# A state-space block with an expert layer: the scan in sub-chunks of 64 tokens, and where B is turned

## What is computed

```python
x = silu(_causal_conv(input_tensor @ Wx.T, conv_w, conv_b))
b = (x @ Wb.T).reshape(bsz, seq, HEADS, STATE)
c = (x @ Wc.T).reshape(bsz, seq, HEADS, STATE)
dt = softplus(x @ Wdt.T + b_dt)
def step(state, inp):
    x_t, b_t, c_t, dt_t = inp
    decay = exp(dt_t * a)[..., None, None]
    state = decay * state + (dt_t[..., None] * b_t)[..., None] * x_t[:, :, None, :]
    return (state, einsum('bhn,bhnp->bhp', c_t, state))
```

## Time and profile before

| | before |
|---|---|
| median of 3 runs | 1219.45 us |
| lowest, highest | 1218.78, 1220.4 us |
| span of the profiled execution | 1219.8 us |
| granted TensorE clock, mean | 1.000 |
| TensorE busy | 1203.0 us, 99% |
| VectorE busy | 951.8 us, 78% |
| GpSimd busy | 791.4 us, 65% |
| ScalarE busy | 714.7 us, 59% |

### The profile page before, as it was taken

The page is one execution under the profiler, slowest core; times in us unless marked ns, Lnnn a source line. Parts: engine busy times, 40 slices in busy tenths (PEclk is TensorE's granted clock), DMA queues, the critical chain, the costliest instruction groups (busy, mean ns, idle before and its releaser), DMA issues.

```text
span 1219.8 us, 30709 instructions
## 1 busy us (share of the span) xinstructions
PE 1203.0 (99%) x11883; PEld 993.8 (81%) x11883; DVE 951.8 (78%) x2027; ACT 714.7 (59%) x1465; POOL 791.4 (65%) x788
## 2 busy tenths in 40 slices
PE   8999999999999999999999999999999999999998
...
GB/s 300 252 343 341 289 242 140 114 136 120 134 140 117 136 126 122 141 129 119 134 135 122 136 124 169 175 156 92 111 91 92 98 87 127 261 324 321 332 332 167
DMA packets 112351, 214.28 MB, mean 176 GB/s; under 512 B 20432, under 2 KB 78544, under 8 KB 107600
## 3 DMA queue, kind: packets, MB, share of 16 engines
...
...
## 4 chain that ended last, share of the span: by engine, by line
PE 86%; DVE 5%; DMA 3%; SPq 2%; ACT 2%; issue 1%; POOL 1%; ACTq 0%; DVEq 0%; POOLq 0%
PE ps L1439 27%; PE ps L1801 10%; PE ps L2311 8%; PE ps L2290 7%; PE ps L2075 6%; PE ps L1520 4%; PE ps L1487 3%; PE ps L2077 3%; PE ps L1546 3%; PE ps L1509 3%; PE ps L1531 2%; PE ps L1560 2%; PE ps L690 1%; PE ps L743 1%; DMA parts_dram<-xn_lo 1%
## 5 line engine op out<-in xcount | busy, mean ns | idle before, releaser
L1395 ACT ACTIVATE decay<-tap,ncum 128x128 f32<-128x128 f32 x344 | 105.7, 392 | 141.4 <-POOL tap L1289 141.4
L1985 POOL DMA_INDIRECT ffn_dram<-ob,idx x64 | 108.4, 1694 | 85.8 <-DVE ob L1904 74.6
L1296 POOL TENSOR_TENSOR x_lo<-x,x_hi 128x512 fp32r<-128x512 f32 x56 | 77.3, 1380 | 104.3 <-ACT x_hi L1368 104.3
L1174 DVE TENSOR_TENSOR x_dt<-ps,dt 128x512 f32<-128x512 f32 x64 | 44.3, 691 | 120.3 <-PE ps L1546 120.3
L2075 PE MATMUL ps<-dn,mid_hi 128*128 128x512 f32 x288 | 104.9, 399 | 0.5 <-DVE moments L1875 0.5
L2033 ACT ACTIVATE mid<-ps,b_up 128x512 f32<-128x512 f32 x96 | 65.9, 690 | 67.2 <-PE ps L1801 56.3
L1439 PE MATMUL ps<-x_hi,w_hi_b 128*128 128x512 f32 x240 | 99.4, 414 | 0.0
L1439 PE MATMUL ps<-x_hi,w_hi_c 128*128 128x512 f32 x240 | 99.3, 414 | 0.0
L2166 POOL TENSOR_SCALAR yc<-yc,gn_scale,gn_shift 128x512 f32<-128x512 f32 x56 | 76.5, 1378 | 33.0 <-DMA yc<-y_dram 32.9
L1439 PE MATMUL ps<-x_lo,w_hi_b 128*128 128x512 f32 x240 | 94.4, 393 | 0.0
L1439 PE MATMUL ps<-x_lo,w_hi_c 128*128 128x512 f32 x240 | 94.2, 393 | 0.0
...
...
## 6 DMA issues: line engine op xcount, KB each, us to landing
...
```

The costliest lines, as they stand in the source:

```text
L1296: nc.gpsimd.tensor_tensor(low, raw, high, ALU.subtract).then_inc(x_lo_ready, 1)
L1395: n = nc.scalar.activation(decay[g % 2][:, h, :], cum_row[g % NR][:, row, :], ACT.Exp, bias=t.ncum[:, g, h:h + 1])
L1985: pool.indirect_dma_start(out=t.ffn_dram, out_offset=bass.IndirectOffsetOnAxis(ap=t.idx[:, e, h * HC + c:h * HC + c + 1], axis=0), in_=ob[ ...
```

## The change

The scan now works in sub-chunks of 64 tokens, two a chunk. Only the two diagonal quarters of a head's 128x128 matrix are left in `scores` and `own_parts`: 16 products of 64 columns each. What the lower quarter carried goes through the state, which steps twice a chunk: `state_mid` after the first half, the other state tile after the second. So `state_parts` runs twice with 64 columns (8 products each), and `update` makes 16 products of 64 rows, one set for each half, into the free half of the scores' banks. On VectorE `mix` becomes one instruction of 512 elements; the four folding instructions become `shrink` (a state tile times decays, both in SBUF) and an addition, once for each half; the two additions into `yb` become one of 512 elements and two of 128.

Order: x of the next chunk is turned at the head of a chunk, B of the next chunk behind the C projection, and `update` of the next chunk follows its scores. On VectorE `weigh_b` is now the last thing in a chunk. `x_dt` has two buffers. The exchange of halves goes away everywhere (`turned_pair` and its uses), as do the split copies in the front; `update` no longer waits for the bit search or the experts' banks. The front gains four products that sum the decays of each half, and cumulates over 64 tokens. `load_cum` issues four DMAs of 128 KB for one of 512 KB, and two more stores fill `cum_half_dram`. The causal mask takes two GpSimd instructions for three, `exp_rows` one ScalarE instruction for two. The first sub-chunk of a sequence needs no state; every other one has state parts, and `update` and the turn of B now also run for the last chunk of a sequence.

```diff
@@ phase_front, TensorE
-            pe.matmul(ps_t[1][:, 0:NT * H], t.ones, flat, start=True, stop=True).then_inc(ten, 1)
+            pe.matmul(ps_t[1][:, 0:NT * H], t.later, flat, start=True, stop=True).then_inc(ten, 1)
+            for j in range(2):
+                for a in range(2):
+                    mm = pe.matmul(ps_dt[a * s.HD:(a + 1) * s.HD, j * NT * MT:(j + 1) * NT * MT],
+                                   t.headavg[:, j * s.HD:(j + 1) * s.HD], dta[:, :, a * MT:(a + 1) * MT],
+                                   start=True, stop=True, skip_group_check=True)
+            mm.then_inc(ten, 1)
             tile(4, range(2, MT))
...
@@ phase_scan, VectorE
+        def shrink(g, j):
+
+            source = (states[g % 2], state_mid)[j]
+            n_scaled[0] += 1
+            dve.wait_ge(state_ready, ends(g)) if j == 0 else dve.wait_ge(mid_ready, g + 1)
+            v.tensor_tensor(state_tmp, source, dec[j][:, g, :].unsqueeze(2).to_broadcast([P, MT, HD]),
+                            ALU.mult).then_inc(scaled, 1)
+
+        def middle_state(g):
+
+            dve.wait_ge(s_mm, g + 1)
+            if g % SPAN == 0:
+                v.tensor_copy(state_mid, ps_new[0]).then_inc(mid_ready, 1)
+            else:
+                dve.wait_ge(scaled, n_scaled[0])
+                v.tensor_tensor(state_mid, ps_new[0], state_tmp, ALU.add).then_inc(mid_ready, 1)
+
+        def end_state(g):
+
+            dve.wait_ge(scaled, n_scaled[0])
+            v.tensor_tensor(states[(g + 1) % 2], ps_new[1], state_tmp, ALU.add).then_inc(state_ready, 1)
 
         def clear_y(g):
 
-
...
+        def add_state_banks(g):
+
+
+            b, c = g // CH, g % CH
             dve.wait_ge(y_mm, g + 1)
             if c == 0:
...
+
+        def add_other_halves(g):
+
+
             dve.wait_ge(y_step, g + 1 + g // SPAN + 1)
-            v.tensor_tensor(y_out, y_1, y_out, ALU.add).then_inc(y_ready, 1)
+            y = y_halves(g)
+            for a in range(2):
+                part = y[:, a, :, (1 - a) * HD:(2 - a) * HD]
+                n = v.tensor_tensor(part, ps_y[1 - a][:, 2 * a * P:2 * (a + 1) * P].rearrange(
+                    "p (r n) -> p r n", r=2)[:, :, (1 - a) * HD:(2 - a) * HD], part, ALU.add)
...
-                    finish(g - 1)
-                clear_y(g)
-            if g == 0:
-                weigh_b(g)
+            if g + 1 < NT:
+                scale_x(g + 1)
+            middle_state(g)
             dve.wait_ge(exp_ready, g + 1)
-            dve.wait_ge(g_ready, g + 1)
-            for i in range(2):
-                v.tensor_tensor(mix[:, 4 * i:4 * i + 4, :],
-                                ps_g[i][:, :].rearrange("p (h n) -> p h n", h=4),
-                                decay[g % 2][:, 4 * i:4 * i + 4, :], ALU.mult).then_inc(mix_ready, 1)
-            if g >= LAST:
-                update(g - 1)
-            elif g % SPAN:
-                finish(g - 1)
-            if g and not last:
-                weigh_b(g)
+            if not last:
+                shrink(g, 1)
+            v.tensor_tensor(mix.rearrange("p (a h) n -> p a (h n)", a=2), ps_scores,
+                            decay[g % 2].rearrange("p (a h) n -> p a (h n)", a=2), ALU.mult).then_inc(mix_ready, 1)
+            if not last:
+                end_state(g)
             if 1 <= g <= ROUNDS:
                 next_bits(g - 1)
+            if LIST0 < g <= LIST1:
+                add_lists(g - 1 - LIST0)
             if LIST0 - 1 <= g < LIST1 - 1:
...
@@ load_cum
     @block.sync
     def _(sp):
         def load_cum(g):
             until(sp, exp_ready, g - NR + 1)
-            sp.dma_start(cum_row[g % NR][:, :, :], t.cum_dram[g].partition_broadcast(P)).then_inc(cum_loaded[g % NR], 16)
+            until(sp, ecum_ready, g - NR + 1)
+            for j in range(2):
+                half = slice(j * HD, (j + 1) * HD)
+                sp.dma_start(key_row[g % NR][half, :, :], t.cum_half_dram[j, g].partition_broadcast(HD)).then_inc(
+                    cum_loaded[g % NR], 16)
+            for a in range(2):
+                half = slice(a * HD, (a + 1) * HD)
+                sp.dma_start(query_row[g % NR][half, :, :],
+                             t.cum_dram[g, a * MT:(a + 1) * MT, :].partition_broadcast(HD)).then_inc(
...
@@ causal
+            pool.wait_ge(cum_loaded[g % NR], 4 * loads(g, NR))
+            row = key_row[g % NR]
+            nc.gpsimd.affine_select(out=row, in_=row, compare_op=ALU.is_ge, fill=-1e30, base=HD,
+                                    pattern=[[0, H], [1, HD]], channel_multiplier=-1).then_inc(row_ready, 1)
             pool.wait_ge(row_ready, 2 * g + 1)
-            nc.gpsimd.affine_select(out=odd[0:HD], in_=odd[0:HD], compare_op=ALU.is_ge, fill=-1e30, base=-HD,
-                                    pattern=[[0, H // 2], [1, P]], channel_multiplier=-1).then_inc(row_ready, 1)
...
@@ TensorE
                 until(pe, b_out, MT * b)
                 until(pe, c_out, MT * b)
-            until(pe, mix_ready, 2 * g)
+            until(pe, mix_ready, g)
+            until(pe, mid_ready, g)
+            until(pe, state_ready, ends(g))
             for m in range(MT):
                 for p, a in ((0, 0), (1, 1), (1, 0), (0, 1)):
-                    n = (m + 2 * p) % MT
-                    r, j = slice(a * HD, (a + 1) * HD), key_half(n // 2, p)
-                    keys = bT[b % 2][r, n, c * P + p * HD:c * P + (p + 1) * HD]
-                    mm = pe.matmul(ps_g[a][p * HD:(p + 1) * HD, n * P + j * HD:(n + 1) * P],
-                                   keys, cT[b % 2][r, n, c * P + j * HD:(c + 1) * P],
-                                   start=True, stop=True)
+                    rows, cols = slice(a * HD, (a + 1) * HD), slice(c * P + p * HD, c * P + (p + 1) * HD)
+                    mm = pe.matmul(ps_g[a][p * HD:(p + 1) * HD, m * HD:(m + 1) * HD], bT[b % 2][rows, m, cols],
+                                   cT[b % 2][rows, m, cols], start=True, stop=True, skip_group_check=True)
...
-            elif g == LAST + 2:
-                pe.wait_ge(x.xg_hi_ready, 2 * s.KT)
-            ps_s = added(g)
+            pe.wait_ge(b_w_ready, g + 1)
             for m in range(MT):
-                for a in range(2):
-                    h, i = (a * MT + m) * HD, (2 * m + a) * HD
-                    mm = pe.matmul(ps_s[a * HD:(a + 1) * HD, m * HD:(m + 1) * HD], b_w[:, i:i + HD],
-                                   x_dt[:, h:h + HD], start=(m == 0), stop=True, skip_group_check=True)
+                for p, a in ((0, 0), (1, 1), (1, 0), (0, 1)):
+                    rows, h, i = slice(p * HD, (p + 1) * HD), (a * MT + m) * HD, (2 * m + a) * HD
+                    mm = pe.matmul(ps_g[p][a * HD:(a + 1) * HD, UPD + m * HD:UPD + (m + 1) * HD],
+                                   b_w[rows, i:i + HD], x_dt[g % 2][rows, h:h + HD], start=True, stop=True,
+                                   skip_group_check=True)
             mm.then_inc(s_mm, 1)
 
         def own_parts(g):
 
 
-            for r, tiles in enumerate(((0, 1), (2, 3), (1, 0), (3, 2))):
+            for q in range(MT):
                 for i, p in ((0, 0), (1, 1), (1, 0), (0, 1)):
-                    q, rows = tiles[p], slice(p * HD, (p + 1) * HD)
-                    h, j = 2 * q + i, key_half(q, p)
-                    mm = pe.matmul(ps_y[p][i * HD:(i + 1) * HD, q * P + j * HD:(q + 1) * P],
-                                   x_dt[rows, h * HD:(h + 1) * HD], mix[rows, h, j * HD:P],
-                                   start=(r == 0), stop=(r >= 2), skip_group_check=True)
+                    h, rows = 2 * q + i, slice(p * HD, (p + 1) * HD)
+                    mm = pe.matmul(ps_y[p][i * HD:(i + 1) * HD, q * P + p * HD:q * P + (p + 1) * HD],
+                                   x_dt[g % 2][rows, h * HD:(h + 1) * HD], mix[rows, h, :],
+                                   start=(q == 0), stop=False, skip_group_check=True)
             return mm
 
-        def state_parts(g):
...
+        def state_parts(g, j):
+
+
+            held = (states[g % 2], state_mid)[j]
             for m in range(0, MT, 2):
                 for i, a in ((0, 0), (1, 1), (1, 0), (0, 1)):
-                    mm = pe.matmul(ps_y[a][i * HD:(i + 1) * HD, q * P:(q + 1) * P], state[r, m + i, :],
-                                   c_dec[r, m + i, :], start=False, stop=True, skip_group_check=True)
+                    r, q = slice(a * HD, (a + 1) * HD), 2 * a + m // 2
+                    mm = pe.matmul(ps_y[a][i * HD:(i + 1) * HD, q * P + j * HD:q * P + (j + 1) * HD],
+                                   held[r, m + i, :], c_dec[r, m + i, j * HD:(j + 1) * HD], start=False, stop=True,
+                                   skip_group_check=True)
             return mm
 
...
                 slots(c)
-            if b + 1 < NB:
+            if g and b + 1 < NB:
                 project(b + 1, c, 1)
+            if more:
+                turn_b(g + 1)
             until(pe, lists_read, listed(g))
-            if g < LAST:
```

(26 more changed lines are left out.)

358 lines of the change are left out of this document (160 added, 198 removed).

## The result

| | before | after |
|---|---|---|
| median | 1219.12 us (4 runs) | 1239.78 us (4 runs) |
| lowest, highest | 1218.35, 1220.4 us | 1237.72, 1241.64 us |
| span of the profiled execution | 1219.8 us | 1235.9 us |
| TensorE, VectorE, GpSimd busy | 1203.0, 951.8, 791.4 us | 1189.5, 1044.4, 774.8 us |

A forecast was written before the change was run, and what follows sets the result against it. TensorE, busy 99% of the span, was taken as the bound, VectorE second. Scan -25.7, front +1.1, bits +4.5, slots +0.5, last four chunks -1.0 sum to -20.6 us: 1198.9, stated 1199.0; 8-in-10 range 1190.5 to 1213.

The forecast's parts named there:

- TensorE, chunk by chunk: TensorE in the scan: 0.52 us less per chunk without lists, 0.39 with lists; -25.7 us after what comes back.
- the rival of 25 ns: TensorE's small products: records do not go below 25 ns, +0.8 us a chunk, total 1268 us; chance 0.03.
- VectorE in the lists: VectorE in list chunks: 6.7 us against TensorE's 8.90, 2.2 to spare, so 1.2 us of GpSimd waits are covered.
- The third rival: VectorE sets the pace of bits and lists: waits of 2.9 us, bits 10.8, lists 9.6, total 1246; chance 0.08.
- Bits and slots: VectorE waits give back time: bit chunks 9.1 us against 8.79, +4.5 us; chunk 17's slots gain nothing, +0.5 us.
- The turn of B "taken at nothing": TensorE's turn of B, moved behind the C projection: costs what it did, 0.44 us, the move itself nothing.
- Last four chunks: End of the scan, 23.43 us before, paced by the loop over both engines: -1.0 us, bounded by -3 and +2.

The follow-up runs named there:

- e1_fold: Changed kernel with both `shrink`-and-add state steps put back to four instructions each, reading the state from SBUF and the update from PSUM: 1207.97 us.
- e16: Kernel before the change, its four-instruction state step written as one product with two SBUF inputs and one add from PSUM: 1243.70 us.
- e3_psum: Changed kernel with one `shrink` operand moved to PSUM, a maximum in place of the product, the state's decay left out: 1209.71 us.
- e5: e1_fold with B turned between the two projections again and `b_w` weighed ahead of bits, lists and statistics: 1249.06 us.
- e9_fold_again: The kernel of e1_fold run again: 1217.17 us, ratio to the kernel before 0.9966.

## Why the prediction was wrong

- **TensorE, chunk by chunk: right.** Without lists 9.09 became 8.53 (forecast 8.57), and where nothing waits a list chunk takes 8.87 in e1_fold (forecast 8.90): -0.42 against -0.39. Groups of four stay at 0.058 through the whole burst; the rival of 25 ns falls.
- **VectorE in the lists: the step that failed.** The prediction took "1.2 us of waits a chunk in all. In the lists that is covered." The trace has 3.1 us a list chunk, more than the 2.2 to spare, and 6.7 of work and 3.1 of waits make the 9.8 that were found. Three parts were wrong. The bound "each can wait between 0 and 1.3 us" assumed one GpSimd instruction; the second `shrink` waits through two (2.08, 0.41 quiet). The partners were others too: the first meets `list_values` and not `c_dec`, the second the mask and `c_dec` and not x_lo. L1019 was not counted in the lists, and costs 1.04. And a share of GpSimd's time (a third) was used as a chance of meeting it, as if the engines ran apart; but the meeting repeats, in most list chunks of the changed kernel and in every second one of e16. The third rival had the mechanism, its condition (2.6 us of waits in the lists) and nearly its price there, 9.6 a chunk; I gave it 0.08. Its bits of 10.8 did not come, so that its total, 1246, lies near 1239.78 in part by luck.
- **The rule of the Trainium skill.** The Trainium skill ("SBUF — State Buffer", Who interferes with whom) puts two SBUF inputs on VectorE against GpSimd instructions that read SBUF. e3_psum turns that rule into an experiment, and agrees: one operand moved to PSUM, 421 ns for 1830 and 30 us less.
- **Bits and slots.** Chunks with statistics took 9.17 (forecast 9.1), but the same in e1_fold, without any `shrink`: there VectorE's order and work set it (8.75 in e5 with the other order), not the waits. Chunks 1, 5 and 16 with 10.60, 10.37 and 10.26 us took back what was gained; in e1_fold they are at 8.78, 8.78 and 8.52, so they belong to `shrink` too.
- **The turn of B "taken at nothing": the place behind C costs nothing that shows, but the other place would.** Between the projections, one chunk ahead, it and the earlier `b_w` cost 41 us against e1_fold and 32 against e9_fold_again; 26.7 us of TensorE's waits there are for ScalarE's copy.
- **Last four chunks: -1.0 forecast, +1.9 found.** One `shrink` of 2.87 us in chunk 61 delays `xg_lo`, for which TensorE waits 3.2 us; it waits through a GpSimd product of 3.44 us and the mask behind it. e1_fold has chunks 60 and 61 at 11.21 against 11.63 before.

```profile
767.40 2.87 DVE L1050 TENSOR_TENSOR decay<-decay,dec 128x256 f32<-128x256 f32 x1
...
770.59 1.27 DVE L1724 TENSOR_TENSOR xg_lo<-ps,xg_hi 128x512 fp32r<-128x512 f32 x2
```

- **A term that the sum lacked: gaps at every 256th record.** They are 10.4 us in e1_fold, where 2.1 were before (9.0 in the changed kernel). Of the 11 us by which the lists of e1_fold exceed the forecast, 7.6 are such gaps; so its 1208 against the forecast of 1199 is mostly that, as near as can be told.
